# A mixture-of-experts stage: the signal for the next expert weights placed behind the gather instead of directly behind the row transfer

## The chip, the cores and the metric

One core of one Trainium2 chip runs the whole kernel. The metric is the device time of one launch in microseconds (us); lower is better. The runs shown are the median of three. The profile is of one further execution, with its own time.

## The reference

The layer takes 2048 tokens of width 512 through local attention, a long convolution and a feed-forward part. Only the last part matters here:

```python
idx, wts = _router(x, gate_w, e_bias)          # 6 of 64 experts for each token
shared = _relu2(x @ shared_up_w.T) @ shared_down_w.T
# routed: every expert takes at most 128 tokens
h = _relu2(einsum('ecd,eid->eci', xd, w1))     # 128 tokens x 512 -> 256
yd = einsum('eci,edi->ecd', h, w2)             # -> 128 x 512
out = zeros.at[tok].add(yd[e, slot] * gate)    # rows added to the tokens' rows
return shared + routed                         # plus the residual
```

## The kernel before, in words

The kernel is written with one instruction stream for each engine and semaphores between them; the order of every queue is written out by hand. After attention, convolution and routing comes the expert stage, a loop over 64 experts in which the work of one expert is spread over all engines.

For expert e (slot s = e mod 8, turn i = e div 8):

- **SyncE** (`load_expert`, L411) loads the expert's 1 MB of weights into a ring of 8 slots. `AHEAD` is 6: the load of expert e waits until `scatter_begun` says that the row transfer of expert e-6 has had its descriptors written (L421, L426).
- **GpSimd** (`gather`, L584) fetches the 128 token rows of an expert (2304 B each, 295 KB in all) from the DRAM tensor `token_rows` with an indirect DMA. 8 slots hold them.
- **TensorE** transposes the rows (`tokens_T`), makes the hidden layer (`hidden`, which waits for the weights at L1633) and the output (`outputs`). In every eight experts it also makes one tile of the shared feed-forward part (`tile_part`).
- **ScalarE** and **VectorE** take the products out of PSUM. VectorE squares the hidden values (L1294), copies the indices of the next transfers (L1319, L1320) and multiplies the expert's rows by their gates into one of `NY` = 4 buffers (L1321), which raises `y_ready`.
- **GpSimd** (`scatter`, L590) adds those 128 rows (2048 B each, 256 KB) to the result in DRAM with an indirect DMA that accumulates. Two such transfers may touch the same row, so each waits until the one before has landed (`pool.wait_ge(added, before)`, L594).

GpSimd's queue therefore holds, for each expert, these in this order: the row transfer of expert n (L596), a product of one column (L601) that raises `scatter_begun` and so lets SyncE ask for the weights of expert n+6, and the gather (L585) of the token rows of expert n+7. The product is there because an arithmetic instruction stands behind the writing of the descriptors. Once in 16 experts a transfer of two finished tiles of the shared part (`scatter_tiles`, L607, 512 KB) stands between two row transfers; it belongs to the same chain of landings. In all there are 64 row transfers and 4 tile transfers. In the last 8 turns of the last group there are no gathers and, since nothing is left to load, the marks release nothing.

Row transfers and gathers are both issued by GpSimd and share one DMA queue (q0, "software_dynamic"); the expert weights, issued by SyncE, have another (q1, "hardware_dynamic"). Both are served by the same 16 DMA engines.

Of the kernel before, what the change touches and what calls it, by code (L numbers as in the profile page):

```python
# [61 lines left out]
def program(nc, a, out):  # L62
# [10 lines left out]
    with ctx:  # L73
# [3 lines left out]
        def sem(name):  # L77
            return ctx.enter_context(nc.semaphore(name))
# [87 lines left out]
        NW, AHEAD = 8, 6  # L166
# [32 lines left out]
        UE, NY = 8, 4  # L199
        GROUP = 2 * UE  # L200
# [71 lines left out]
        scatter_begun = sem("scatter_descriptors_written")  # L272
# [84 lines left out]
        @block.sync  # L357
        def _(sp):
            sp.dma_start(X[:, 0:4, :], a["x"][0:4 * P, :].rearrange("(t p) d -> p t d", p=P)).then_inc(x_loaded, 16)

            def load(dst, name, s):
                sp.dma_start(dst, a[name]).then_inc(s, 16)

            load(wq, "wq", w_loaded)
            load(wkv, "wkv", w_loaded)
            load(rope, "rope", tables_loaded)
            load(bias, "bias", tables_loaded)
            load(bo, "bo", tables_loaded)
            load(wo, "wo", tables_loaded)
            load(kpad[:, P:], "kern", small_loaded)  # L370
            load(dcol[:], "skip", small_loaded)

            for s in (*empt, *conv_used, *conv_filled, *y_filled, *y_ready, hsq_ready, tile_ready):
                sp.sem_inc(s, 1)
            sp.sem_inc(scatter_landed, 5)
            sp.sem_inc(conv_done, 2)
            sp.sem_inc(x_loaded, 16)

            sp.wait_ge(tables_loaded, 16 * 4)
            with sp.Fori(1, PAIRS) as i:  # L380

                sp.wait_ge(x_loaded, i * 16 + 16)
                sp.dma_start(X[:, ds(i * 4, 4), :],
                             a["x"][ds(i * (4 * P), 4 * P), :].rearrange("(t p) d -> p t d", p=P)).then_inc(x_loaded, 16)

            sp.wait_ge(consts_ready, 1)
            sp.dma_start(out[T:ROWS, :], zeros[:]).then_inc(zero_written, 16)
            sp.dma_start(xrows[T:ROWS, 0:D], zeros[:]).then_inc(zero_written, 16)
            sp.dma_start(xrows[T:ROWS, D:XW], zeros[:, 0:E]).then_inc(zero_written, 16)
            sp.wait_ge(pad_ready, 1)  # L390
            sp.dma_start(toep[:], kpad[:]).then_inc(toep_written, 16)

            sp.wait_ge(full[FA1.bank(("vmid",))], FA1.filled(("vmid",)))
            sp.wait_ge(toep_written, 16)
            toep_v = bass.AP(toep.tensor, 1, [[P + D, SH], [1, P], [1, D]])
            with sp.Fori(0, SH // NTR) as i:
                for s in range(NTR):

                    sp.wait_ge(conv_filled[s], i + 1)
                    sp.wait_ge(toep_written, 16)  # L400
                    sp.dma_start(tring[:, s:s + 1, :], toep_v[ds(i * NTR + s, 1), :, :].rearrange("h p d -> p h d"))\
                      .then_inc(head_loaded[s], 16)
                    sp.dma_start(cring[:, s, :, :].rearrange("p m i -> p (m i)"),
                                 a["ctxE"][ds((i * NTR + s) * P, P), :]).then_inc(head_loaded[s], 16)

            for k, t in enumerate(TILES3):
                sp.wait_ge(x3_ready[k % NX], k // NX + 1)
                sp.dma_start(xrows[t * P:(t + 1) * P, 0:D], x3[:, k % NX, :]).then_inc(x3_written[k % NX], 16)
            sp.wait_ge(gates_ready, 1)
            sp.dma_start(xrows[0:T, D:XW].rearrange("(t p) c -> p t c", p=P), W).then_inc(gates_written, 16)  # L410
            def load_expert(s, i):  # L411
                sp.dma_start(wring[s], a["wexp"][ds((i * UE + s) * P, P), :]).then_inc(wexp_loaded[s], 16)

            for s in range(UE):
                if s == 4:

                    sp.wait_ge(upper_written, 16)
                if s == 6:
                    sp.wait_ge(full[FS.bank(("dn", 1, 3))], FS.filled(("dn", 1, 3)))
                if s >= AHEAD:  # L420
                    sp.wait_ge(scatter_begun, s - AHEAD + 1)  # L421
                load_expert(s, 0)
            with sp.Fori(1, E // UE) as i:
                for s in range(UE):

                    sp.wait_ge(scatter_begun, i * UE + (s - AHEAD + 1))  # L426
                    load_expert(s, i)

            sp.wait_ge(added, 16 * (E + NT // 4))
# [3 lines left out]
        def _(pool):  # L433
# [150 lines left out]
            def gather(s):  # L584
                pool.indirect_dma_start(xg[:, s, :], None, xrows, bass.IndirectOffsetOnAxis(ap=idxg[:, s:s + 1], axis=0))\  # L585
                    .then_inc(xg_loaded[s], 16)
# [3 lines left out]
            def scatter(s, i, before):  # L590

                pool.wait_ge(y_ready[s % NY], i * (UE // NY) + (s // NY + 2))
                if before is not None:
                    pool.wait_ge(added, before)  # L594
                    pool.sem_inc(scatter_landed, 1)
                pool.indirect_dma_start(out, bass.IndirectOffsetOnAxis(ap=idxs[:, s % NY:s % NY + 1], axis=0),  # L596
                                        ysb[:, s % NY, :], None, compute_op=ALU.add).then_inc(added, 16)

                if before is not None:
                    pool.wait_ge(scatter_begun, i * UE + s)  # L600
                G.tensor_tensor(begun_mark[:], minus_half[:, 0:1], minus_half[:, 0:1], ALU.mult).then_inc(scatter_begun, 1)  # L601

            def scatter_tiles(j):
                pool.wait_ge(tile_ready, j + 2)
                pool.wait_ge(added, j * (16 * LINKS) + 16 * (GROUP - 1))
                pool.sem_inc(scatter_landed, 1)
                pool.indirect_dma_start(out.rearrange("(r g) d -> r (g d)", g=2),  # L607
                                        bass.IndirectOffsetOnAxis(ap=idxt[:, 0:1], axis=0),
                                        ytile.rearrange("p g d -> p (g d)"), None, compute_op=ALU.add)\
                    .then_inc(added, 16)  # L610
# [5 lines left out]
            pool.wait_ge(upper_written, 16)  # L616
            pool.wait_ge(out_written, 16 * 2)
            scatter(0, 0, None)

            def group(j, more):  # L620
                for r in range(GROUP):
                    n = r + 1
                    if n == GROUP - 1:
                        scatter_tiles(j)
                    if n < GROUP:
                        scatter(n % UE, j * 2 + n // UE, j * (16 * LINKS) + 16 * (n if n < GROUP - 1 else n + 1))
                    elif more:
                        scatter(0, j * 2 + 2, j * (16 * LINKS) + 16 * LINKS)
                    if more or r < UE:
                        gather(r % UE)  # L630

            with pool.Fori(0, last) as j:
                group(j, True)
            group(last, False)

        @block.scalar
# [1116 lines left out]
```

## Time and profile before

| What | us |
|---|---|
| median of 3 runs | 989.93 |
| lowest and highest | 986.37 and 991.56 |
| the profiled execution's own time | 993.13 |
| its span in the profile | 991.3 |
| TensorE busy in the span | 893.3 |
| GpSimd busy in the span | 464.1 |

The span is what the trace covers, from the first instruction to the last; 1.8 us of the profiled execution lie outside it. The expert stage fills its last 430 us or so. PE is TensorE's matmuls, PEld its weight loads, DVE VectorE, ACT ScalarE, POOL GpSimd and SP SyncE. A DMA issued by an instruction runs on after it: the duration shown for a DMA_INDIRECT on POOL is the writing of its descriptors.

### The profile page before, as it was taken

What the parts mean: (1) busy time and instruction counts of PE and PEld (TensorE: products, weight loads), DVE (VectorE), ACT (ScalarE), POOL (GpSimd) and SP (SyncE); (2) the same over time, 40 slices, a digit from 0 to 9 for tenths busy, and PEclk for the clock granted to TensorE, in tenths of its full rate; (3) what the DMA queues carried; (4) which work ended last, traced back from release to release, by engine and by line L of the source; (5) the groups of instructions that cost most, each with busy time, mean ns of one, the idle gap of its engine ahead of it and who ended that gap; (6) DMA issues with size and microseconds to landing.
All of it is one profiled execution on the core that took longest, in us unless ns stands there. A gap on an engine that the chain in (4) does not pass through costs nothing. (4 is left out here: it accounts for less than half of the span.)

```text
span 991.3 us, 14544 instructions
## 1 busy us (share of the span) xinstructions
PE 893.3 (90%) x4913; PEld 627.6 (63%) x4913; DVE 551.9 (56%) x1143; ACT 232.5 (23%) x716; POOL 464.1 (47%) x512
## 2 busy tenths in 40 slices
PE   4799999988899999869999999999999799898980
PEld 3566666664677777766444486867676567575840
DVE  4788888867688888886889422323222222131220
ACT  1465656461400000113110021111121111111200
POOL 1644452533588888630183323554454454444422
PEclk9989999999999999979999999999999899899995
DMA  7300000020533333033006558898988889889853
GB/s 291 112 1 2 1 2 1 2 75 1 199 112 96 97 99 95 0 118 138 0 1 226 187 162 259 258 273 236 276 264 237 221 252 277 269 227 278 267 122 53
DMA packets 44125, 143.40 MB, mean 145 GB/s; under 512 B 7280, under 2 KB 11632, under 8 KB 35120
## 3 DMA queue, kind: packets, MB, share of 16 engines
q1 hardware_dynamic: 26352, 96.46, 26.4%
q0 software_dynamic: 14912, 37.76, 19.3%
q10 hardware_dynamic: 2816, 8.59, 2.3%
q8 instruction: 27, 0.44, 0.2%
q14 instruction: 18, 0.15, 0.0%
HBM read 114.36 MB, written 28.43 MB: 144 GB/s over the span
## 5 line engine op out<-in xcount | busy, mean ns | idle before, releaser
L1359 PE MATMUL ps<-arena 128*128 128x128 f32 (+4 forms) x2128 | 521.4, 403 | 11.6 <-DVE arena L813 5.7
L1359 PEld LDWEIGHTS ps<-arena 128*128 128x128 f32 x2128 | 342.2, 193 | 154.0 <-issue 107.6
L596 POOL DMA_INDIRECT out<-arena,scatter_rows x64 | 102.0, 1594 | 216.7 <-DMA out<-arena,scatter_rows 147.2
L1294 DVE TENSOR_TENSOR arena<-arena 128x256 f32<-128x256 f32 x64 | 27.4, 427 | 222.1 <-ACT arena L798 215.9
L1359 PE MATMUL ps<-features_T,arena 128*128 (+2 forms) x640 | 116.0, 338 | 0.0
L646 ACT ACTIVATE arena<-ps 128x512 f32<-128x512 f32 (+1 forms) x137 | 78.4, 591 | 129.0 <-DVE residual L1258 56.8
L1359 PEld LDWEIGHTS ps<-features_T,arena 128*128 128x128 f32 x640 | 84.7, 188 | 37.3 <-issue 37.3
L468 POOL TENSOR_TENSOR arena<-arena 128x512 f32<-128x512 f32 x48 | 49.2, 1057 | 87.4 <-DVE arena L833 87.4
L585 POOL DMA_INDIRECT arena<-token_rows,gather_rows x64 | 66.3, 1037 | 38.2 <-DVE gather_rows L1287 27.1
L798 ACT ACTIVATE arena<-ps 128x256 f32<-128x256 f32 x64 | 24.5, 383 | 248.8 <-PE ps L1359 247.1
L656 ACT ACTIVATE arena<-arena 128x128 f32<-128x128 f32 x192 | 74.0, 389 | 16.6 <-DVE arena L821 16.3
L521 POOL TENSOR_TENSOR arena<-arena 128x512 f32<-128x512 f32 x32 | 40.7, 1272 | 43.2 <-DVE arena L1079 43.1
L1628 PEld LDWEIGHTS ps<-ident,arena 128*128 128x128 f32 x256 | 31.1, 143 | 43.3 <-DMA arena<-token_rows,gather_rows 23.1
L1666 PE MATMUL ps<-arena 128*128 128x512 f32 x128 | 57.5, 592 | 0.0
L1628 PE MATMUL ps<-ident,arena 128*128 128x128 f32 x256 | 39.8, 279 | 15.7 <-DMA arena<-token_rows,gather_rows 15.6
L601 POOL TENSOR_TENSOR begun_mark<-minus_half 128x1 f32<-128x1 f32 x64 | 51.1, 799 | 0.0
L1321 DVE TENSOR_SCALAR arena<-ps,arena 128x512 f32<-128x512 f32 x64 | 47.9, 749 | 0.5 <-issue 0.3
L1319 DVE COPY scatter_rows<-slot_rows_u 128x1 uint32 (+1 forms) x64 | 9.8, 154 | 64.2 <-PE ps L1359 59.7
L1666 PEld LDWEIGHTS ps<-arena 128*128 128x128 f32 x128 | 24.3, 190 | 30.6 <-issue 30.6
L756 ACT ACTIVATE arena<-features_T 128x256 f32 x32 | 13.0, 416 | 122.0 <-DVE arena L1079 119.8
L1086 DVE TENSOR_REDUCE arena<-arena 128x1024 f32 (+1 forms) x32 | 38.7, 1208 | 0.0
L656 ACT ACTIVATION_READ_ACCUMULATOR arena<-arena 128x1 f32 x192 | 36.3, 189 | 0.0
(174 smaller groups left out, 1069.3 us busy)
## 6 DMA issues: line engine op xcount, KB each, us to landing
arena<-wexp SPq DMA_DIRECT2D x48, 1024.0 KB
residual<-wexp SPq DMA_DIRECT2D x16, 1024.0 KB
arena<-toeplitz_rows SPq DMA_DIRECT2D x32, 256.0 KB, 3.1
arena<-ctxE SPq DMA_DIRECT2D x32, 192.0 KB, 3.2
residual<-x SPq DMA_DIRECT2D x4, 1024.0 KB, 5.4
token_rows<-arena SPq DMA_DIRECT2D x16, 256.0 KB, 2.0
arena<-suT ACTq DMA_DIRECT2D x1, 2048.0 KB, 7.7
arena<-sdT ACTq DMA_DIRECT2D x1, 2048.0 KB, 12.6
```

The source lines that it names most:

```text
L468: G.tensor_tensor(e, e, rinv[:, b, 4 * c:4 * c + 4, q:q + 1].broadcast_to((P, 4, P)), ALU.mult)\
L521: G.tensor_tensor(halfsum[:, s % 2].rearrange("p m j k -> p (m j) k"), pv[:, :, 0:4], pv[:, :, 4:8], ALU.add).then_inc(half_ready, 1)
L585: pool.indirect_dma_start(xg[:, s, :], None, xrows, bass.IndirectOffsetOnAxis(ap=idxg[:, s:s + 1], axis=0))\
L596: pool.indirect_dma_start(out, bass.IndirectOffsetOnAxis(ap=idxs[:, s % NY:s % NY + 1], axis=0), ysb[:, s % NY, :], None, compute_op=ALU.a ...
L601: G.tensor_tensor(begun_mark[:], minus_half[:, 0:1], minus_half[:, 0:1], ALU.mult).then_inc(scatter_begun, 1)
L646: A.activation(dst, src, ACT.Copy, **kw).then_inc(empt[bank], 1)
L656: ins = A.activation(prob[:, b, k, q, :], prob[:, b, k, q, :], ACT.Exp, bias=negmax[:, b, k, q:q + 1], scale=1.0, accum_out=rowsum[:, b, k ...
L1086: V.tensor_reduce(o[:, 0:2 * B, :], prodb[:, s % 2, 0:2 * B], axis=AX.X, op=ALU.add)
L1321: V.tensor_scalar(ysb[:, s % NY, :], ps[:, 4 + s % 2, :], xg[:, s, ds(i * UE + (D + s), 1)], None, ALU.mult)\
L1359: ins = TE.matmul(out_ap, lhsT, rhs, start=(n == 0), stop=(n == len(pairs) - 1))
L1628: ins = TE.transpose(ps[:, bank, c * P:(c + 1) * P], xg[:, s, c * P:(c + 1) * P], ident[:])
L1666: ins = TE.matmul(ps[:, 7, :], htile[:, k, :], sdT[:, k, :], start=(k == 0), stop=(k == 7))
```

## The change

The product leaves `scatter` and becomes a function of its own, `ask_for_weights`, which is called after the gather. So GpSimd's order for each expert becomes: row transfer, gather, product. The counting semaphore starts one higher (`sp.sem_inc(scatter_begun, 1)`), and every wait on it counts one higher, so that each weight load still belongs to the same row transfer. The wait that kept two products apart goes with the product. No work is added or removed.

```diff
@@ SyncE
+            sp.sem_inc(scatter_begun, 1)
...
                 if s >= AHEAD:
-                    sp.wait_ge(scatter_begun, s - AHEAD + 1)
+                    sp.wait_ge(scatter_begun, s - AHEAD + 2)
                 load_expert(s, 0)
...
-                    sp.wait_ge(scatter_begun, i * UE + (s - AHEAD + 1))
+                    sp.wait_ge(scatter_begun, i * UE + (s - AHEAD + 2))
                     load_expert(s, i)
@@ GpSimd, in scatter
                                         ysb[:, s % NY, :], None, compute_op=ALU.add).then_inc(added, 16)
-                if before is not None:
-                    pool.wait_ge(scatter_begun, i * UE + s)
+            def ask_for_weights(n):
+                pool.wait_ge(scatter_begun, n)
                 G.tensor_tensor(begun_mark[:], minus_half[:, 0:1], minus_half[:, 0:1], ALU.mult).then_inc(scatter_begun, 1)
...
             scatter(0, 0, None)
+            ask_for_weights(1)
@@ GpSimd, in group
                     if more or r < UE:
                         gather(r % UE)
+                    if n < GROUP or more:
+                        ask_for_weights(j * GROUP + (n + 1))
```

## Rows read from the trace of the kernel before

**Rows 1.** The page: busy time by engine; DMA busy in 40 slices.

```profile
PE 893.3 (90%) x4913; PEld 627.6 (63%) x4913; DVE 551.9 (56%) x1143; ACT 232.5 (23%) x716; POOL 464.1 (47%) x512
...
DMA  7300000020533333033006558898988889889853
```

**Rows 2.** Waits of POOL, 579 to 991 us: total us, times, longest.

```profile
POOL out L596 <- DMA out<-arena,scatter_rows: 147.2, 48, 6.9
...
POOL out L596 <- DVE arena L1321: 22.1, 3, 13.5
```

**Rows 3.** Timeline of POOL: first and last row transfers (start, us, [idle before <-releaser]).

```profile
579.78 1.62 POOL L596 DMA_INDIRECT out<-arena,scatter_rows  x1 [13.50 <-DVE arena L1321]
...
945.30 1.58 POOL L596 DMA_INDIRECT out<-arena,scatter_rows  x1 [5.79 <-DMA out<-arena,scatter_rows]
...
950.78 1.56 POOL L596 DMA_INDIRECT out<-arena,scatter_rows  x1 [3.69 <-DMA out<-arena,scatter_rows]
...
978.25 1.56 POOL L607 DMA_INDIRECT out<-arena,tile_scatter_rows  x1 [3.79 <-DMA out<-arena,scatter_rows]
984.99 1.55 POOL L596 DMA_INDIRECT out<-arena,scatter_rows  x1 [5.19 <-issue]
```

**Rows 4.** Timeline of POOL: one usual turn.

```profile
624.94 1.58 POOL L596 DMA_INDIRECT out<-arena,scatter_rows  x1 [2.54 <-DMA out<-arena,scatter_rows]
625.96 0.78 POOL L601 TENSOR_TENSOR begun_mark<-minus_half 128x1 f32<-128x1 f32 x1
626.90 1.03 POOL L585 DMA_INDIRECT arena<-token_rows,gather_rows  x1 [0.16 <-issue]
630.44 1.58 POOL L596 DMA_INDIRECT out<-arena,scatter_rows  x1 [2.51 <-DMA out<-arena,scatter_rows]
```

**Rows 5.** Timeline of SP in the same turn.

```profile
626.91 0.35 SPq L412 DMA_DIRECT2D residual<-wexp  x1
```

**Rows 6.** Windows of that turn: last two columns are DMA share and GB/s.

```profile
627.04:628.94 1.90, 1.90 (x19) 1.90 (x18) 0.00 (x0) 0.39 (x1) 0.89 (x1) 1.00 1.05 123
628.94:629.34 0.40, 0.40 (x3) 0.16 (x2) 0.00 (x0) 0.21 (x1) 0.00 (x0) 1.00 1.26 400
629.34:631.44 2.10, 2.10 (x12) 1.33 (x11) 0.83 (x4) 0.67 (x2) 1.00 (x1) 1.00 1.00 423
631.44:632.44 1.00, 1.00 (x11) 1.00 (x10) 1.00 (x2) 0.00 (x0) 1.00 (x2) 1.00 0.83 331
```

**Rows 7.** DMA queues, 629.34 to 630.94 us: packets, MB, share of 16 engines.

```profile
q1 hardware_dynamic: 82, 0.67, 99.0%
```

**Rows 8.** Timeline of POOL: a long turn.

```profile
742.23 1.58 POOL L596 DMA_INDIRECT out<-arena,scatter_rows  x1 [2.53 <-DMA out<-arena,scatter_rows]
...
751.50 1.58 POOL L596 DMA_INDIRECT out<-arena,scatter_rows  x1 [6.28 <-DMA out<-arena,scatter_rows]
```

**Rows 9.** DMA queues, 746.63 to 748.23 us, in the long turn.

```profile
q1 hardware_dynamic: 68, 0.56, 89.1%
q0 software_dynamic: 7, 0.01, 4.2%
```

**Rows 10.** DMA queues, 583.35 to 583.75 us, in the first turn.

```profile
q1 hardware_dynamic: 3, 0.02, 17.8%
```

**Rows 11.** Timeline of POOL: gathers behind gathers, before the stage.

```profile
559.08 0.95 POOL L585 DMA_INDIRECT arena<-token_rows,gather_rows  x1 [0.30 <-issue]
```

**Rows 12.** One line of the source, L495: a one-column product elsewhere (min/median/max ns).

```profile
L495 POOL TENSOR_TENSOR padded_kernels<-padded_kernels,skip_gain x1: 179/179/179, 43.4 to 43.4; 32x1 f32<-32x1 f32 x1
```

**Rows 13.** Timeline of DVE: the last expert's rows.

```profile
962.66 0.74 DVE L1321 TENSOR_SCALAR arena<-ps,arena 128x512 f32<-128x512 f32 x1
```

**Rows 14.** Waits of PEld, 620 to 970 us: total us, times, longest.

```profile
PEld ps L1628 <- DMA arena<-token_rows,gather_rows: 23.1, 12, 6.5
```

**Rows 15.** Windows: PE busy over its part of the stage.

```profile
573.00:960.50 387.50, 370.47 (x2145) 272.50 (x2145) 103.02 (x279) 65.48 (x143) 173.84 (x179) 0.98 0.84 245
```

## The prediction

> **What bounds the kernel now.** The page comes first. TensorE is busy for 90% of the span and GpSimd for 47%, which points to TensorE; but the DMA digits stand at 8 and 9 through the last third, where the change lies [rows 1]. So the next view is the waits of POOL in that stage: the row transfer (L596) waits 147.2 us in 48 waits for the landing of the row transfer before it, and only 3 times for VectorE's rows [rows 2]. The reader is to see that the chain is not the engines' work but landing after landing. The timeline of POOL bears it out: from the first row transfer at 579.78 to the last at 984.99 us there are 67 steps, of which the ones shown are typical: idle until the landing before, or nearly [rows 3]. This chain, 405.2 us, sets the end.
>
> TensorE isn't far behind it. In its 387.5 us of the stage it is busy 370.5 [rows 15]. Its last rows are finished at 962.66 + 0.74 = 963.4 [rows 13], and their transfer is issued at 984.99 [rows 3]: 21.6 us of slack at the end. That is the room that a faster chain has before TensorE's end becomes the limit.
>
> **How long is a step?** After 945 us neither gathers nor weights run, but for one last load. From 950.78 to 978.25 there are five steps, 27.47 / 5 = 5.49 us each; the tile transfer's step is 984.99 - 978.25 = 6.74 [rows 3]. From 579.78 to 945.30 there are 60 steps in 365.5 us. Three are tile steps of the kind shown, 6.7 to 7.0 us each (20.5 us together) and the first is 7.5 us, since it waits for VectorE. The other 56 share 337.5 us: 6.03 each. So a step beside gathers and weights costs 0.53 us more than one alone, 30 us over the 56. What the change can win or lose is in these 30 us, and in whether the 5.49 stays.
>
> **Where the 0.53 comes from.** I take a usual turn, the row transfer issued at 624.94 and the next one 5.50 later [rows 4], and ask for the DMA's share in windows. Rows run on the engines from about 2.1 to 4.0 us after the issue (share 1.05 at 123 GB/s; shares above 1 are packets that overlap). The weights follow at 423 GB/s, and last comes the gather, which is over by 7.5 us, some 0.1 us before the next transfer's rows can start at 5.50 + 2.1 = 7.6 [rows 6]. In the middle of the weights' stretch q1 has the engines alone, 99.0% [rows 7]. Adding up: 1.9 x 1.05 + 0.4 x 1.26 + 2.1 x 1.00 + 1.0 x 0.83 = 5.43 us of DMA work in a step of 5.50. The engines are full, with the slack of a tenth or a few tenths of a us.
>
> So an engine that falls behind stays behind. Compare the same stretch (4.4 to 6.0 us after the issue) of a long turn, 742.23 to 751.50, 9.27 us [rows 8]: 68 packets of q1 and 7 of q0 [rows 9]. Row packets of this transfer are still waiting on a late engine while the weights run on it, and they come one at a time in 1.6 us; 7 packets of 0.18 us would need 1.3 us if they followed each other. I read this as row packets that alternate with weight packets: each left-over row packet pays for an 8 KB weight packet (0.67 MB in 82 packets that fill 16 engines for 1.6 us: 1.6 x 16 / 82 = 0.31 us). A late engine with eight rows left would add up to 8 x 0.31 = 2.5 us to the landing that the chain waits for. In the order of before, a late engine has the gather in front of its rows, in the same queue, and the weights of this turn beside them.
>
> The Trainium skill ("DMA: Bandwidth & Descriptors", section on queues, rings and completion order) says that a DMA engine goes round between the queues it has work for, packet by packet, a packet being some 9 to 17 descriptors. By it a whole share of weights (82 packets seen in 1.6 us on 16 engines, about 8 for each in a load) would pass at once, so that a late engine would lose 2.5 us or nothing. Rows 9 look finer than that; the sum would be the same in its upper bound.
>
> **The change part by part.** Nothing is computed anew; two instructions change places, 56 times with a gather between them.
>
> *The gather moves forward.* Before, the product starts 1.02 us after the transfer and lasts 0.78, and the gather starts at 1.96 [rows 4]. Without the product between them the gather starts at the earliest where the product did, 1.02 + 0.16 = 1.18, and at the latest as a gather does behind another DMA, 0.30 after its end [rows 11], at 1.58 + 0.30 = 1.88. I take 1.88: a one-column product alone takes 0.18 [rows 12], so its 0.78 behind the transfer is mostly waiting for the descriptors, and so would the gather's be. The gather thus gains 0.1 us of issue, at most 0.8. The larger shift is in the queue: its packets now stand directly behind the rows in q0, at about 4 us instead of 6.5.
>
> *The product moves back.* It ends 0.22 us after the descriptors of what stands before it (1.80 against 1.58 [rows 4]). Behind the gather (1.04 long) it ends at 1.88 + 1.04 + 0.22 = 3.14, or 2.44 with the early gather, against 1.80: SyncE's request, which follows the product within 0.2 us [rows 4, 5], comes 1.34 us later (0.64 at least). The first weight packets were seen 3.6 us after a transfer's issue [rows 10]; they now come at 4.9 (4.2). SyncE has nothing else queued behind this wait. Behind the product on POOL stands only the next transfer, which waits until 5.5 anyway; at 3.14 the product is covered by 2.3 us.
>
> *The order on the engines* is then rows (to 4.0), gather (0.8 us of share, to 4.8), weights (2.5 to 2.6 us, from 4.9 to 7.5), and the next rows at 7.6. For an engine in time this costs and gives nothing. For a late engine two things differ: its rows come directly behind the last weights, not behind weights and gather; and the weights of the turn reach it 0.6 to 1.3 us later, when 3 to 7 more row packets of 0.18 us are gone. A lateness up to 0.7 us or so, which now makes alternating packets, would then make none.
>
> *The sum.* Upper bound of the gain: all 30 us. Lower bound: the weights end too close to the next rows. If they start at 5.4 rather than 4.9, they end at 7.9 to 8.0 and push the rows of the next turn by 0.3 to 0.4; that turn then starts its own chain later and absorbs it, so about 0.2 us for each of 56 turns, 11 us lost. I take half of the 30 us, 15 us, nearer to the upper bound than to the lower one, because the order leaves no bubble by the rows above, while lateness that has other causes (the 9 us turn lost more than the 2.5 us of one share) will partly stay. 993.1 - 15 = 978.1 for an execution like the profiled one, which lies 3.2 us above the median shown: 975 us.
>
> **TensorE.** It waits 23.1 us in 12 waits (of the weight loads) for gathered rows [rows 14]. These get earlier by 2 us or more. The weights come later by about 1.0 us (their end 7.5 against 6.5), and TensorE needs both for the next expert but one or so; the later of the two is then about where it was (7.5). I cost this at nothing: TensorE's slack is 21.6 us at the end. If the cover were gone, 0.3 us for each expert would be 19 us of TensorE and still fit in it, barely.
>
> **Rivals.**
>
> *Half or more of the long turns go* (the forecast): 0.52 for a result between 963 and 984.
>
> *Everything goes, and TensorE becomes the limit.* The chain would be 56 x 0.53 = 30 us shorter, but the slack allows 21.6 plus what TensorE itself gains: 966 or a little below. For it: TensorE's waits for gathers go. Against: the DMA is full. 0.14.
>
> *The saturated DMA takes it back; no change.* The 5.43 us of DMA work in 5.50 is the same in any order, and lateness might come from the memory side and not from alternation; then 989 to 990. For it: shares of 0.8 to 0.9 all through. 0.19.
>
> *The weights come too late and the stage slows.* One mechanism: the weights' last packets stand in front of the next transfer's rows. It decides from a start of the weights 5.0 us after the issue, where their 2.6 us no longer fit before 7.6. With a product that ends 0.5 us later than I take, 11 us are lost: 1001. The same place would also make TensorE wait at L1633. Against: my figures leave 0.1 us at least, 0.8 with the early gather. 0.15.
>
> **The numbers.** A measurement of this kernel can tell 0.5%, 5 us, from no change: faster is under 985. The forecast and the second case make 0.66; no change 0.19; slower 0.15. The range goes from 961, just under the TensorE limit, to 996, which takes in the unchanged case and the first part of the slow one; it leaves out about 0.17. The likeliest case has 963 to 984.
>
> **What would show it.** Right: the product (now in a line of its own) ends 3.1 us after its transfer; in the windows of a turn the order is rows, gather, weights; steps of the chain average 5.7 to 5.8 between the first transfer and the last gather, with few above 7 us; TensorE waits less for gathered rows. Wrong: weights that start after 5.0 us and steps of 5.8 to 6.0 without long ones (slow case), or long turns as before (alternation was not the cause); or rows that end later than 4.0 us after their issue in a turn without lateness, because the gather's packets stand in the same queue.

## The result: slower by 2.4%

| | before | after |
|---|---|---|
| median, us | 990.74 | 1017.72 |
| lowest and highest | 986.37 to 1002.47 | 1016.16 to 1020.05 |
| span of the profiled execution | 991.3 | 1016.9 |

The ratio is 1.0243, with a 95% interval of 1.020 to 1.0285 (the two medians of the table divide to 1.027, inside it). The forecast was 975 us, with 0.66 for faster; the rival in which the weights come too late had 0.15.

The page of the changed kernel: busy time by engine, DMA in 40 slices, and the two queues.

```profile
PE 900.3 (89%) x4913; PEld 632.8 (62%) x4913; DVE 552.0 (54%) x1143; ACT 232.7 (23%) x716; POOL 460.6 (45%) x512
...
DMA  7300000020533332042008489888999789979853
...
q1 hardware_dynamic: 26352, 96.46, 26.6%
q0 software_dynamic: 14912, 37.76, 20.2%
```

The engines do nearly the same work as before [rows 1]. The chain of landings is again what POOL waits for; for VectorE's rows it waits as little as before [rows 2]. The waits of POOL, 582 to 1017 us, then the first and last members of the chain in its timeline:

```profile
POOL out L597 <- DMA out<-arena,scatter_rows: 156.9, 48, 7.4
...
POOL out L597 <- DVE arena L1326: 22.1, 3, 13.5
```

```profile
582.61 1.61 POOL L597 DMA_INDIRECT out<-arena,scatter_rows  x1 [13.50 <-DVE arena L1326]
...
967.23 1.58 POOL L597 DMA_INDIRECT out<-arena,scatter_rows  x1 [2.77 <-DMA out<-arena,scatter_rows]
976.41 1.56 POOL L597 DMA_INDIRECT out<-arena,scatter_rows  x1 [7.37 <-DMA out<-arena,scatter_rows]
981.93 1.55 POOL L597 DMA_INDIRECT out<-arena,scatter_rows  x1 [3.74 <-DMA out<-arena,scatter_rows]
...
1004.03 1.55 POOL L609 DMA_INDIRECT out<-arena,tile_scatter_rows  x1 [3.92 <-DMA out<-arena,scatter_rows]
1010.56 1.55 POOL L597 DMA_INDIRECT out<-arena,scatter_rows  x1 [4.98 <-issue]
```

The chain is 1010.56 - 582.61 = 428.0 us long, against 405.2 [rows 3]: 22.7 of the 25.6 us by which the span grew. (The first transfer is issued 2.8 us later than in the profile of before. Nothing ahead of it was changed, and in the profiles of the runs below it lies between 579.6 and 588.7.) Where no gathers run, the step is still 5.5 us: (1004.03 - 976.41) / 5 = 5.52, against 5.49 [rows 3]. Beside gathers and weights, the 56 ordinary steps average 6.33 us, against 6.03. The last rows of VectorE are finished at 991.0 and transferred at 1010.56, so TensorE still isn't the limit.

The landing of row transfers (L597, from issue), first line of before (L596), second of after:

```profile
DMA to landing us min/median/max: 4.4/4.8/9.1
```

```profile
DMA to landing us min/median/max: 4.4/5.3/8.4
```

The longest is no longer; the usual one is 0.5 us longer. But more of the 56 steps are long: 10 last over 7 us, against 6 before.

One turn of the changed kernel in the timeline of POOL, then SP's load in it:

```profile
690.51 1.57 POOL L597 DMA_INDIRECT out<-arena,scatter_rows  x1 [2.26 <-DMA out<-arena,scatter_rows]
692.38 1.17 POOL L586 DMA_INDIRECT arena<-token_rows,gather_rows  x1 [0.30 <-issue]
693.58 0.20 POOL L603 TENSOR_TENSOR begun_mark<-minus_half 128x1 f32<-128x1 f32 x1
696.25 1.58 POOL L597 DMA_INDIRECT out<-arena,scatter_rows  x1 [2.48 <-DMA out<-arena,scatter_rows]
698.13 1.02 POOL L586 DMA_INDIRECT arena<-token_rows,gather_rows  x1 [0.30 <-issue]
699.18 0.20 POOL L603 TENSOR_TENSOR begun_mark<-minus_half 128x1 f32<-128x1 f32 x1
```

```profile
693.95 0.34 SPq L413 DMA_DIRECT2D arena<-wexp  x1
```

The instructions stand where the prediction put them: gather 1.88 us after the transfer, product finished at 699.18 + 0.20 - 696.25 = 3.13 (3.14 forecast). SyncE's load is issued 3.3 us after the transfer in most turns (3.44 in the one shown), against 1.97 [rows 4, 5]. What went wrong lies in the DMA engines. The windows of that turn (last two columns: DMA share, which is a sum of packet durations, and GB/s):

```profile
692.61:694.51 1.90, 0.91 (x6) 0.70 (x7) 0.04 (x1) 0.00 (x0) 1.14 (x2) 1.00 1.04 298
694.51:695.91 1.40, 1.40 (x15) 1.40 (x15) 0.00 (x0) 0.00 (x0) 0.00 (x0) 1.00 0.97 222
695.91:698.11 2.20, 2.20 (x9) 0.89 (x8) 0.42 (x1) 0.87 (x2) 1.58 (x1) 1.00 1.01 354
698.11:699.31 1.20, 0.55 (x4) 0.31 (x4) 1.01 (x3) 0.00 (x0) 1.16 (x2) 1.00 1.06 323
```

In this turn the engines see rows, then the gather (694.51 to 695.91), then the weights: the forecast order. But the gather moves only 222 GB/s with the engines full (0.97). Before, in the second half of a turn, it moved 331 GB/s at a share of 0.83 [rows 6]. The weights therefore reach the engines fully at 5.4 us after the issue, not at 4.9. The last window is the place that decides, because there the next rows want the engines. The queues from 2.1 to 3.3 us after the issue of the next transfer, changed kernel, 698.35 to 699.55:

```profile
q0 software_dynamic: 48, 0.10, 61.3%
q1 hardware_dynamic: 41, 0.21, 42.5%
```

and the kernel before, 632.54 to 633.74 (2.1 us after the transfer at 630.44 [rows 4]):

```profile
q0 software_dynamic: 80, 0.17, 108.6%
```

In the turn of before, the next rows had the engines to themselves. In the changed one, 41 weight packets of the old turn stand beside 48 row packets. The stage as a whole shows the same. I counted in the packet records of both traces, over 46 turns without a tile transfer, which packets of the old turn are still at work 2.15 to 3.5 us after the next issue:

| kernel | weight packets | gather packets |
|---|---|---|
| before | 2.5 | 4.1 |
| changed | 26.8 | 0.3 |

One of the signs that were to show the forecast right also failed: TensorE's weight loads don't wait less for gathered rows (24.5 us in 10 waits from 620 to 970 us, against 23.1 in 12 [rows 14]).

### The profile page after: what moved, and what is told of

It reads as the page before. It is cut to its first block and busy times, and to the rows that moved or that the text cites. A ratio compares the mean times of both kernels' runs of the same rounds, so it can differ in the third digit from the quotient of the medians.

```text
span 1016.9 us, 14538 instructions
## 1 busy us (share of the span) xinstructions
PE 900.3 (89%) x4913; PEld 632.8 (62%) x4913; DVE 552.0 (54%) x1143; ACT 232.7 (23%) x716; POOL 460.6 (45%) x512
## 5 line engine op out<-in xcount | busy, mean ns | idle before, releaser
L1364 PE MATMUL ps<-arena 128*128 128x128 f32 (+4 forms) x2128 | 521.9, 404 | 24.3 <-issue 14.1
L597 POOL DMA_INDIRECT out<-arena,scatter_rows x64 | 100.9, 1576 | 233.4 <-DMA out<-arena,scatter_rows 156.9
L803 ACT ACTIVATE arena<-ps 128x256 f32<-128x256 f32 x64 | 24.5, 383 | 272.4 <-PE ps L1364 262.1
L1364 PE MATMUL ps<-arena,residual 128*128 128x128 f32 x256 | 35.1, 295 | 2.9 <-issue 2.9
```

The source lines that it names most:

```text
L1364: ins = TE.matmul(out_ap, lhsT, rhs, start=(n == 0), stop=(n == len(pairs) - 1))
```

## The experiments

Each run was measured beside the kernel before on the same chip. Ratios are to that, with 95% intervals. "Load at" is the time from the start of a row transfer to SyncE's load, in the profile of that run.

**1. The lateness without the change of order, at three sizes.** The kernel before, with the product made wider. The gather stays behind it, so the load becomes late and the order rows, weights, gather stays. The gather's issue moves back by as much, from 1.96 to 2.39 us in the run of 256 columns, so these runs don't tell a late load from a late gather.

```diff
-        begun_mark = sb("begun_mark", [P, 1])
+        begun_mark = sb("begun_mark", [P, 256])      # 96, 256, 768
...
-                G.tensor_tensor(begun_mark[:], minus_half[:, 0:1], minus_half[:, 0:1], ALU.mult)...
+                G.tensor_tensor(begun_mark[:], minus_half[:, 0:1].broadcast_to((P, 256)), (the same), ALU.mult)...
```

256 columns:

> The kernel before, with the product that lets SyncE ask made 256 columns wide instead of one, so that it ends some 0.3 to 0.45 us later; the gather stays behind it and moves by as much. Theory A (the engines' time per turn is what counts: in the changed kernel the gather's packets, directly behind the rows, take 0.28 us each instead of 0.18, which adds 0.4 us of engine time to a turn): the weights start about when the rows end, so this costs little, 985 to 993 us. Theory B (what counts is only how late the weights are asked for, 27 us for 1.34 us): 0.4 / 1.34 of the loss, 996 to 1000 us.

768 columns:

> The kernel before, with that product 768 columns wide, so that it ends 1.0 to 1.5 us later, about where it ends in the changed kernel, but with the gather still behind the weights. Theory B: as slow as the changed kernel, 1015 to 1020 us. Theory A: the engines now stand idle between rows and weights for up to 0.9 us, which the gather fills in the changed kernel, and the gather still comes last; slower than the changed kernel if the idle time is larger than the 0.4 us that the slow gather packets cost: 1020 to 1040 us, with gather packets of 0.18 us.

96 columns (run later, to fill the curve):

> The kernel before with the product 96 columns wide: the load at about 2.1 to 2.2 us instead of 1.98. If the engines have a slack of 0.1 to 0.3 us in a turn, as the windows of the kernel before say: 1.0 to 1.01. If the turn has none: half of the loss of the 256-column run, 1.012.

| columns | load at, us | ratio |
|---|---|---|
| 1 (before) | 1.97 | 1 |
| 96 | 2.14 | 1.0095 (1.005 to 1.014) |
| 256 | 2.40 | 1.024 (1.018 to 1.030) |
| 768 | 3.25 | 1.0225 (1.016 to 1.029) |
| changed kernel | 3.3 | 1.0243 (1.020 to 1.0285) |

The run of 256 columns in the timelines of POOL and of SP:

```profile
701.14 1.58 POOL L596 DMA_INDIRECT out<-arena,scatter_rows  x1 [3.05 <-DMA out<-arena,scatter_rows]
702.17 1.19 POOL L601 TENSOR_TENSOR begun_mark<-minus_half 128x256 f32<-128x256 f32 x1
703.53 1.02 POOL L585 DMA_INDIRECT arena<-token_rows,gather_rows  x1 [0.17 <-issue]
```

```profile
703.54 0.34 SPq L412 DMA_DIRECT2D arena<-wexp  x1
```

Both theories missed a size. The loss isn't in proportion to the lateness (theory B gave 996 to 1000 us for 256 columns; 1023 was measured), and it isn't cheap up to 0.4 us either (theory A gave 985 to 993). 0.17 us already costs 1%, 0.43 us cost all of it, and a further 0.85 nothing more. (In the profile of the run with 96 columns the ordinary steps average 6.00 us, as before; its chain is 3.3 us longer in the steps of the tile transfers, so the 1% rests on the times alone.) The run of 768 columns is the one to compare with the changed kernel: the load is as late, the gather comes last instead of first, and the time is the same. But what is left over for the next rows isn't: by the count of above it is 25.1 gather packets and 7.2 weight packets in a turn here, and 0.3 and 26.8 in the changed kernel.

**2. The same pair with engines that aren't full.** The load brings only W1 of each expert (512 KB); W2 is not loaded, so the expert outputs are not the reference's.

```diff
-                sp.dma_start(wring[s], a["wexp"][ds((i * UE + s) * P, P), :])...
+                sp.dma_start(wring[s][:, 0:1024], a["wexp"][ds((i * UE + s) * P, P), 0:1024])...
```

The kernel before:

> The kernel before, but each expert's load brings only the first half of its weights (512 KB, W1; W2 stays what is in the slot), which frees about 1.3 us of each DMA engine in every turn. Theories A and B: the DMA engines are no longer full, steps fall to 5.5 us or to what TensorE allows, 960 to 975 us.

The changed kernel:

> The changed kernel with the same half loads (W2 is not loaded). Theories A and B (the loss comes only from full DMA engines): within 5 us of the half-load kernel before. Theory C (the loss comes from something else: TensorE waiting for later weights, or GpSimd's order itself): still 15 to 27 us slower than that.

Measured: 971.91 us (0.9723, 0.966 to 0.978) and 974.68 us (0.9747, 0.970 to 0.980). The change costs 2.8 us here instead of 27, and the two intervals overlap. Theory C falls: neither TensorE's wait for later weights nor GpSimd's order costs much by itself. (A half load is also over sooner than a whole one. For TensorE's part the waits of POOL in the full pair say the same: 22.1 us for VectorE's rows, before and after.) The ordinary steps average 5.54 and 5.64 us, so half the weights also bring the unchanged kernel back to the 5.5 us of a transfer alone. By the count of above, 0.4 and 4.9 weight packets are left over for the next rows. The queues in the pages of the two, before and after:

```profile
q0 software_dynamic: 14912, 37.76, 20.0%
q1 hardware_dynamic: 26352, 62.91, 18.9%
```

```profile
q0 software_dynamic: 14912, 37.76, 22.0%
q1 hardware_dynamic: 26352, 62.91, 18.8%
```

The durations of the same packets and bytes of q0 add up to 0.220 x 977.2 = 215.0 us for each engine instead of 0.200 x 970.0 = 194.0: 21 us, or 0.37 us in each of 56 turns. It is the gather's packets that got longer. Most of this doesn't need the rows in front of them. Ahead of the stage the kernel before makes eight gathers in a row, and in this stretch nothing else is on the engines. The queues from 559 to 565 us:

```profile
q0 software_dynamic: 373, 1.35, 79.2%
```

0.792 x 6.0 = 4.75 us for 1.35 MB is 1.04 us for a gather of 295 KB. In the packet records a gather packet (4608 B, four for each engine) averages 0.247 us there, 0.180 behind the weights and 0.284 in the changed kernel. So the gather was cheapest behind the weights, and a line of the trace of before could have told it. The usual packet takes 0.178 us in all three; a part of them takes longer. In the full pair q0 goes from 0.193 x 991.3 = 191.3 to 0.202 x 1016.9 = 205.4 us (14.1 more), and q1 from 261.7 to 270.5 (8.8 more).

**3. The load too early.** The product goes, GpSimd raises the count itself (a semaphore increment instead of an instruction of arithmetic), and the load's time is set by where it does so and by how often SyncE raises a spare semaphore first.

```diff
@@ in scatter; ahead of the transfer
+                pool.sem_inc(scatter_begun, 1)
                 pool.indirect_dma_start(out, ...)
-                G.tensor_tensor(begun_mark[:], ...).then_inc(scatter_begun, 1)
@@ SyncE, k times (none, 20, 40, 44, 51)
                     sp.wait_ge(scatter_begun, ...)
+                    for _ in range(k):
+                        sp.sem_inc(pause, 1)
```

> No product at all: GpSimd raises the count itself just before it starts the row transfer, so SyncE asks 1.8 us earlier than in the kernel before, and the gather starts at 1.88 us directly behind the transfer. Theory A (an engine serves what arrives first, and alternates packet by packet when rows and weights are both queued): the weights arrive at 1.9 us, beside the rows at 2.1, each row packet pays for a weight packet, rows end 2.5 us later: steps of 7 to 8 us, over 1060 us. Theory B (only lateness of the weights costs): not slower than the kernel before, 0.97 to 1.0 of it.

> As the last one, but SyncE raises a spare semaphore 20 times between its wait and the load, which I put at 30 to 60 ns each, so the weights arrive at about 2.5 to 3.1 us. Theory A: part of the rows is already in the engines, a part alternates: between the kernel before and the last one, 1.0 to 1.05 of the kernel before. Theory B: 0.97 to 1.0 of it.

> The same with 40 times: the weights arrive at about 3.1 to 4.3 us (3.6 in the kernel before). Both theories: at 3.6 us about as fast as the kernel before, 0.985 to 1.01 of it; if it is over 4.0 us, 1.02 of it, as with the product of 256 columns.

> The same with 44 times (0.057 us each by the last two runs), so that SyncE's load is issued 2.0 us after the transfer as in the kernel before, with the gather at 1.88. Theory A (what arrives when decides): as fast as the kernel before, 0.99 to 1.01 of it. If raising a semaphore on SyncE costs by itself, 1.01 to 1.02, as with 40 times.

> With 51 times: the load is issued 2.4 us after the transfer, as with the product of 256 columns (1.024), but the gather, at 1.88, arrives before it and stands directly behind the rows as in the changed kernel. Theory A (gather packets behind rows take 0.28 us instead of 0.18): 1.02 to 1.03, with a gather share like the changed kernel's. Theory D (only the end of the turn's last packet before the next rows counts, and the gap of 0.4 us is filled by the gather here): 1.00 to 1.015.

With the count raised between the transfer and the gather, 14 and 24 times:

> No product; GpSimd raises the count between the row transfer and the gather, and SyncE raises a spare semaphore 14 times (0.057 us each) before the load. The load should be issued about 2.0 us after the transfer, as in the kernel before, and the gather at 1.88. Theory A (what arrives first at the engines decides): weights first, gather packets of 0.18 us, 0.99 to 1.01 of the kernel before.

> With 24 times: the load at about 2.5 us, so that the gather, issued at 1.88, comes first. Theory A (gather packets directly behind the rows cost 0.4 us of engine time in a turn): 1.02 to 1.03, though its weights come no later than in the run with the product of 256 columns. Theory D (a gap filled by the gather costs nothing; only weights later than the gather's end do): 1.00 to 1.01.

And with the count raised behind the gather, without a product:

> The changed kernel without its product: GpSimd raises the count itself behind the gather, so the load is issued at about 2.9 to 3.0 us instead of 3.3. If the lateness of the weights behind the gather matters: 1.012 to 1.02. If only the order rows, gather, weights matters: 1.024, as the changed kernel.

| run | load at, us | ratio |
|---|---|---|
| none, ahead | -0.57 | 1.050 (1.039 to 1.060) |
| none, behind the gather | 0.47 | 1.102 (1.094 to 1.110) |
| 20, ahead | 0.63 | 1.123 (1.113 to 1.133) |
| 14, between | mostly 1.3 to 1.6, some from 0.8 | 1.073 (1.063 to 1.083) |
| 40, ahead | mostly 1.8 to 2.2, one in eight at 3.3 to 7.7 | 1.017 (1.007 to 1.027) |
| 24, between | 1.8 to 2.4, mostly 2.0, at most 3.4 | 1.001 (0.997 to 1.006) |
| 44, ahead | 2.4 to 3.6, a quarter at 4.2 to 11 | 1.044 (1.038 to 1.050) |
| 51, ahead | 2.8 to 4.4, one in ten at 5.4 to 7.5 | 1.034 (1.028 to 1.040) |

The run with the count behind the gather didn't do what it was made for: the load is issued 0.47 us after the transfer, ahead of the gather that stands before the count in the queue. Timelines of POOL and SP:

```profile
717.61 1.58 POOL L596 DMA_INDIRECT out<-arena,scatter_rows  x1 [5.03 <-DMA out<-arena,scatter_rows]
719.49 1.02 POOL L585 DMA_INDIRECT arena<-token_rows,gather_rows  x1 [0.30 <-issue]
725.59 1.57 POOL L596 DMA_INDIRECT out<-arena,scatter_rows  x1 [5.08 <-DMA out<-arena,scatter_rows]
```

```profile
718.08 8.32 SPq L412 DMA_DIRECT2D arena<-wexp  x2
```

Its queues from 3.0 to 4.5 us after the transfer, when the rows should be at work, and from 5.0 to 6.5, when they should be gone:

```profile
q1 hardware_dynamic: 73, 0.60, 99.1%
```

```profile
q0 software_dynamic: 158, 0.35, 109.0%
q1 hardware_dynamic: 13, 0.01, 1.7%
```

The weights go first, all of them, and the rows wait: the first row packet of a turn starts 4.8 us after the issue (median; 2.15 in the kernel before). Most turns last 7.7 to 8.0 us, and the median landing is 7.0 us instead of 4.8 (7.2 in the run with 20). A whole share of weights in front of the rows, eight packets of 0.31 us, costs an engine the same 2.5 us as eight row packets that each pay for a weight packet, so the size of the loss doesn't tell the two apart; the queues do, and here the rows don't alternate with the weights. The expected place between the kernel before and the earliest load was wrong for the run with 20: it is the worst of all. With the load at -0.57 the weights also go first, but they are through sooner (first row packet at 3.5 us, against 5.1 in the run with 20).

In the run with 24 the gather is issued at 1.88 without a product before it, and the load as in the kernel before. It was meant to bring the gather in front of the weights, with the load at 2.5, and missed that: the load came at 2.0, and the middle one of the gather's packets still starts 6.7 us after the transfer, behind the weights. So it shows that the early issue costs nothing and gives nothing, and says nothing on the gather's place. The runs with 44 and 51 missed their load times (2.0 and 2.4 were meant), so they don't tell the theories apart; they only say that a load mostly at about 3.3 or 3.9 us, with some far later, is slow here too. The 1.7% of the run with 40 is no cleaner: its usual load is at 1.8 us, near the 1.97 of before, but the late ones are in it too.

**4. The gather first, the load less late.** The same with 32 and 38 times between.

> As the run with 24 times, but 32: the load at about 2.4 to 2.6 us, the gather at 1.88. Theory A (the gather's slow packets behind the rows cost by themselves): slower than 1.024, the ratio of the run with the product of 256 columns, and gather packets of 0.25 us or more. Theory D (only the load's lateness costs): 1.02 to 1.025, with whichever order.

> With 38 times: the load at about 2.8 us, so that the gather is surely first. Theory A: 1.025 to 1.035. Theory D: 1.02 to 1.025.

Measured: 1.030 (1.024 to 1.036) and 1.041 (1.034 to 1.049). The load again lies late and spread: some at 2.2 to 2.9, most between 3.1 and 4.0 us, and about one in six or seven later, up to 8.1 (32 times) and 9.4 us (38). The gather packets are long, though less than in the changed kernel: they average 0.258 us in the run with 32, against 0.201 in the run of 256 columns and 0.284. The ratio is on theory A's side of the two, but with load times that spread this much it isn't proof.

## Why the prediction was wrong

**The bound and the place** were right: the chain of landings set the end before and after, TensorE's slack at the end (21.6 us, now 19.6) was never used, and all of the loss but the 2.8 us of a later start lies in the chain.

**The instructions** came where they were forecast: gather at 1.88, product to 3.13, load 1.3 us later.

**The step that failed** is in "the order on the engines": "rows (to 4.0), gather (0.8 us of share, to 4.8), weights (2.5 to 2.6 us, from 4.9 to 7.5), and the next rows at 7.6. For an engine in time this costs and gives nothing." Two terms of it were mis-sized.

- The gather's 0.8 us of share was read where the gather follows the weights. Directly behind the rows its packets last 0.37 us more in a turn, as the half-load pair shows. So the order does change the sum of the packets' durations, which I took as the same 5.43 us for any order.
- The slack that I allowed ("a tenth or a few tenths of a us") is not there. A load and gather 0.17 us later cost 1%, 0.43 us later 2.4%. What is late in one turn stands beside the rows of the next: 26.8 weight packets in a turn instead of 2.5. The price isn't in proportion to the packets, since the run of 256 columns leaves over about half as many (13.9, with 7.0 gather packets) and loses as much.

**The gain** that I set against it was half of the 30 us by which steps beside gathers and weights exceed 5.49. Rows that pay for weights of their own turn are real. In the long turn of [rows 8] the last row packets start at 747.13, 747.61, 748.09, 748.56 and 749.04 us, 0.476 us apart, the length of one row packet and one weight packet, and with half the weights nearly all of the 30 us goes. The early loads show weights of the turn in front of its rows costing up to 2.4 us a turn, though there a whole share passes first, the other way in which the prediction thought it might be. But a later load doesn't avoid the meeting. It moves it from the end of this turn's rows to the start of the next turn's, and there it meets many engines, not the late ones alone. The longest landings got no longer (8.4 against 9.1) while the median rose by 0.5.

**The rival** "the weights come too late" named this place, and its condition, weights from 5.0 us on, is what the windows show (5.4 in the turn shown). It gave 1001 us. Its price was too low, because I let the next turn absorb the push; the 56 steps lost 0.30 us each (17 us), and the rest of the 22.7 lies in the tile steps and in the last step with weights (9.18 us, from 967.23, against 5.48 from 945.30).

**What stays open** is how the loss divides. Lateness with the gather last (768 columns) costs as much as lateness with the gather first. In the first case it is mostly the late gather that stands beside the next rows, in the second the late weights, so the equal times don't say what the gather's place costs or saves by itself. It may take back what it would save by filling the idle time between rows and late weights: 0.37 us of longer gather packets is most of the time that they could fill. That was argued and not shown, since the runs made to separate the two had load times that spread.

No version beat the kernel before. Along the load's time it stands at the best place that was found: about 1.4 us is too early (1.073), 2.14 too late (1.0095, with the gather as much later), and 24 times between (about 2.0) gives the same time.

## What to carry to other kernels

Where transfers fill the DMA engines and one of them is a chain, the order of the requests is a schedule: read for each transfer when the engines get it and what stands beside the chain's next one, and take no slack below a few tenths of a us for granted. Moving a bulk load away from one critical transfer moves it towards the next; check the other end of the gap with the same care. And a transfer's engine time isn't its own property: read it in the place to which it goes, or bound it from both sides.

## What was unexpected of the hardware

- The packets of the same gather last longer behind the rows than behind a bulk load: 0.37 us more in a turn of 295 KB. Behind neither they are nearly as long (0.247 us on average, against 0.284 and 0.180).
- Rows and weights meet in two ways. In the long turn row packets start 0.476 us apart, as if they alternated with weight packets; in the run without a product, where the weights are asked for at 0.47 us, the weights pass as a whole before the first row.
- GpSimd's semaphore raise doesn't wait for the descriptor writing in front of it: placed behind a gather that starts at 1.88 us, it released SyncE's load at 0.47; placed between transfer and gather, it let SyncE's row of raises begin 0.2 us before the start that the trace shows for the transfer. The one-column product, an instruction of arithmetic, did wait: it ends 0.2 us after the descriptors in both kernels.
- A row of semaphore raises on SyncE is a poor clock. The raises follow each other at 0.058 us, but with pauses of 0.3 to 0.7 us in between: on average 0.75 us of them in a row of 24 raises, 1.45 in one of 38, yet only 0.28 in the run with 40. In the runs with 32, 38, 44 and 51 the load mostly came at 3.1 to 3.9 us and in some turns far later. The runs with 32 and more also load more of the program (51 or 52 packets in queue q14, against 18 to 21), but the run with 40 does so too, so the cause stays open.
